# One attention kernel: value products of two key tiles issued together, every fourth score step, in the cosine half

## What is computed

```python
xn = layernorm(x)                                   # (2, 1024, 128), 16 heads of 8
q, k = l2norm(xn @ Wq.T), l2norm(xn @ Wk.T)         # cosine: every key counts
out = softmax(g_scale * q @ k.T) @ (xn @ Wv.T)
...
q, k = rope(rms(xn) @ wq), rope(rms(xn) @ wk)       # causal: 16 query, 4 key heads
out = softmax(mask(q @ k.T / sqrt(8))) @ (rms(xn) @ wv)
```

## Time and profile before

| | |
|---|---|
| Median of three runs | 706.77 us |
| The profiled execution, as a run | 705.19 us |
| Its span in the trace | 703.5 us |
| TensorE matmul busy | 620.3 us (88%) |
| ScalarE busy | 461.6 us (66%) |
| VectorE busy | 367.0 us (52%) |
| GpSimd busy | 103.9 us (15%) |
| Mean granted TensorE clock | 0.966 of 2.4 GHz |

### The profile page before, as it was taken

One profiled execution on the slowest core, in us unless ns is written; L12 is line 12 of the kernel. 1 busy time (PEld: TensorE's weight loads), 2 busy tenths in 40 slices (PEclk: granted clock), 3 DMA queues, 4 the chain that ended last, 5 costly groups with the idle time before them and its releaser, 6 DMA issues.

```text
span 703.5 us, 11087 instructions
## 1 busy us (share of the span) xinstructions
PE 620.3 (88%) x4068; PEld 272.4 (39%) x4068; DVE 367.0 (52%) x1042; ACT 461.6 (66%) x520; POOL 103.9 (15%) x245
## 2 busy tenths in 40 slices
PE   0661789999999999999999999999998689999996
PEld 0331223333333333333333333333333445556654
DVE  6577565555547465555555654655521534344333
ACT  1344548888889888888888888988988342222221
POOL 8245000210210210030021021021002200000000
PEclk9976779999999999999999999999999889999999
DMA  3015100320311302123332030221000000000000
GB/s 84 4 17 88 31 16 16 48 41 7 62 16 31 54 9 47 28 36 76 114 54 35 13 62 11 36 46 18 1 3 1 1 0 1 15 1 16 0 16 15
DMA packets 19189, 20.61 MB, mean 29 GB/s; under 512 B 8128, under 2 KB 15552, under 8 KB 19136
## 3 DMA queue, kind: packets, MB, share of 16 engines
q1 hardware_dynamic: 16736, 19.62, 15.9%
q10 hardware_dynamic: 2400, 0.30, 0.3%
HBM read 3.84 MB, written 1.05 MB: 7 GB/s over the span
## 4 chain that ended last, share of the span: by engine, by line
PE 78%; DVE 14%; ACT 5%; issue 2%; DMA 1%; SPq 0%; POOL 0%; DVEq 0%; ACTq 0%
PE ps L1050 27%; PE ps L1031 19%; PE ps L982 6%; PE ps L1127 6%; PE ps L1113 5%; PE ps L1114 5%; PE ps L1011 3%; DVE neg_piece L719 2%; DVE masked_scores L715 2%; PE ps L1005 2%; ACT probs L583 2%; DVE out_t L795 2%; DMA x_tok<-in_x 1%; DVE probs L692 1%; DVE probs L681 1%
## 5 line engine op out<-in xcount | busy, mean ns | idle before, releaser
L583 ACT ACTIVATE probs<-ps 128x1024 f32<-128x1024 f32 (+2 forms) x416 | 395.5, 991 | 77.6 <-PE ps L1031 73.4
L715 DVE CUSTOM_DVE_ANT_0 masked_scores<-ps,mask_q 128x384 bf16<-128x384 f32 (+3 forms) x256 | 111.6, 488 | 75.8 <-PE ps L982 75.3
L1050 PE MATMUL ps<-probs,v_cos_pad 128*32 128x512 f32 x1024 | 139.0, 615 | 0.0
L1031 PE MATMUL ps<-q_cos_t,k_cos_t 64*128 64x512 f32 x512 | 124.2, 482 | 16.6 <-DVE parts_rope L703 14.7
L1031 PEld LDWEIGHTS ps<-q_cos_t,k_cos_t 64*128 64x128 f32 x512 | 48.8, 188 | 137.4 <-ACT probs L583 74.5
L502 POOL TENSOR_SCALAR_AFFINE_SELECT probs<-probs 128x512 f32<-128x512 f32 x64 | 40.3, 635 | 413.6 <-ACT probs L583 413.6
L719 DVE TENSOR_REDUCE neg_piece<-ps 128x1 f32<-128x512 f32 x128 | 82.2, 685 | 20.3 <-PE ps L982 20.3
L621 ACT ACTIVATE probs<-ps 128x512 f32<-128x512 f32 x48 | 28.5, 597 | 96.3 <-PE ps L1114 84.9
L982 PE MATMUL ps<-k_causal_t,q_causal_t 33*128 33x512 f32 (+3 forms) x384 | 65.3, 378 | 19.9 <-DVE neg_piece L719 10.6
L1050 PE MATMUL ps<-probs,v_causal_pad 128*32 128x512 f32 (+3 forms) x768 | 81.6, 498 | 0.3 <-POOL probs L502 0.3
L1031 PE MATMUL ps<-q_causal_t,k_causal_t 64*128 64x512 f32 (+3 forms) x384 | 73.2, 406 | 3.2 <-ACT probs L583 3.2
(11 more groups left out here) (129 smaller groups left out, 412.6 us busy)
## 6 DMA issues: line engine op xcount, KB each, us to landing
q_cos_t<-parts_t_cos SPq DMA_DIRECT2D x64, 64.0 KB
q_causal_t<-parts_t_rope SPq DMA_DIRECT2D x64, 64.0 KB
k_cos_t<-parts_t_cos SPq DMA_DIRECT2D x32, 64.0 KB
k_cos_t<-parts_t_cos SPq DMA_DIRECT2D x64, 32.0 KB
parts_cos<-in_w SPq DMA_DIRECT2D x2, 768.0 KB, 5.6
x_tok<-in_x SPq DMA_DIRECT2D x4, 256.0 KB, 4.4
k_causal_t<-parts_t_rope SPq DMA_DIRECT2D x16, 64.0 KB
k_causal_t<-parts_t_rope SPq DMA_DIRECT2D x32, 32.0 KB
```

The lines of the kernel that those rows point to most:

```text
L583: act.activation(step_probs(n), step_scores(n), ACT.Exp).then_inc(probs_ready, 1)
L715: ins = dve.tensor_tensor_reduce(out=masked_scores[:, head % 2, at:at + keys], in0=scores, in1=mask_q[:, BANK - keys:BANK], scale=-1.0, sc ...
L1031: ins = pe.matmul(slot(n)[:, i, at:at + width], rounded(keys[:, j * P:(j + 1) * P]), rounded(queries[:, q0:q0 + width]), start=True, stop= ...
L1050: ins = pe.matmul(acc[32 * h:32 * h + 32, lo:], v, unit_probs(n)[:, h, lo:], start=j == 0, stop=True, skip_group_check=True)
```

## The change

`unit_steps` gives two consecutive cosine units (an even one and the odd one after it) the same step: two after the last score step of the odd one. `UNITS_AT` then holds a list of units for a step, and the loops of TensorE and VectorE go through the list. In every iteration the cosine pairs are due at relative steps 5, 9, 13, 17, 21, 25, 29 and 33. The causal units keep their steps, as do all jobs and `copy_sums` (steps 17 and 33 in the cosine). No instruction is added or removed on any engine; TensorE's order alone is another.

```diff
     for n in range(iters * UNITS_AN_ITERATION):
         it, u = divmod(n, UNITS_AN_ITERATION)
         step = it * STEPS + LAST_STEP[u] + (3 if on_diagonal(u) else 2)
-        if n:
+        if UNITS[u][0] == COS:
+            step = it * STEPS + LAST_STEP[u - u % 2 + 1] + 2
+        if n and not (UNITS[u][0] == COS and u % 2):
             step = max(step, at[-1] + (3 if UNITS[u][2] == 0 else 1))
         at.append(step)
...
-UNITS_AT = {step: n for n, step in enumerate(UNIT_STEP)}
+UNITS_AT = {}
+for _n, _step in enumerate(UNIT_STEP):
+    UNITS_AT.setdefault(_step, []).append(_n)
...
-                if n in UNITS_AT and UNITS_AT[n] % UNITS_AN_ITERATION in LAST_OF_HALF:
-                    copy_sums(UNITS_AT[n])
+                for u in UNITS_AT.get(n, []):
+                    if u % UNITS_AN_ITERATION in LAST_OF_HALF:
+                        copy_sums(u)
...
-                if n in UNITS_AT:
-                    value_unit(UNITS_AT[n])
+                for u in UNITS_AT.get(n, []):
+                    value_unit(u)
```

## The result

The changed kernel takes 740.36 us (median of four runs, 738.65 to 743.33) against 707.19 for the kernel before (median of four): a ratio of 1.0475, 95% interval 1.0441 to 1.051. It is slower by 33 us, where 742 was forecast. The profiled execution is the longest of the four, 743.33 us with a span of 741.6, so the two traces lie 38.1 us apart (703.5 before) where the medians lie 33 apart.

What follows compares the result with a forecast made beforehand. TensorE and ScalarE were taken to hold each other, with ScalarE's cover by two score slots too short for a pair. Iterations adding +27.5, +5.3 and +2.8 gave +35.6 us: 740.8 profiled, 742 median, range 734 to 754.

Steps and rivals of the forecast that it cites:

- The period: Four cosine score steps with one pair, replayed from the first scores after a pair: 4.92 us from start to start.
- idle time at a pair: ScalarE's wait from its last ready exponential to the first one after a pair: 1.14 us.
- the periods with transpositions: Four-step periods from step 22, with step 24's two transpositions, 5.45 us; from step 26, with jobs between scores, 5.13 us.
- The hold of a pair: Time two adjacent cosine value units keep TensorE from the next scores: 1.89 to 1.98 us, 1.90 used.
- The cover: ScalarE's ready work at a pair's start: 1.79 us from the start of scores 4, against 2.93 needed.
- the rival with TensorE as the pace: TensorE sets the pace and saved tiling-mode switches win 11.5 us: 695 us; chance 4%.
- The sums: Added time over all iterations: +27.5, +5.3 and +2.8 us, with 0 for the first iteration's early steps; together +35.6.
- Iterations 1 to 6: Steps 5 to 34 take 37.51 us against 32.92: +4.59 each, +27.5 in six.
- The last: Last iteration, which prepares no further queries and keys: 37.30 us against 31.96, +5.3.
- The first, from step 17: First iteration, steps 17 to 34: 22.3 us against 19.54, +2.8.
- Its steps 3 to 17: First iteration's early steps, paced by VectorE and partly at 1.2 GHz: change taken as 0, from -3 to +6 us.
- The clock: Rival: new TensorE gaps drop the clock to 1.2 GHz once per iteration, adding 27 us: 769 us; chance 8%.

Runs made afterwards that it cites:

- the catching up at step 7: Kernel before with single units re-placed by ScalarE's cover, two of them due together at step 7: 701.68 us; 700.57 us with the first iteration's order kept.

## Why the prediction was right

- **The period.** Worked out 4.92 us, measured 4.88; idle time at a pair 1.14 against 1.10; the periods with transpositions 5.45 against 5.41 (361.25 to 366.66 in the trace) and 5.13 against 5.02 (366.66 to 371.68). The order of steps in it, TensorE held by the pair, then ScalarE awaited twice, is that of the trace.
- **The hold of a pair.** 1.90 was taken between 1.89 and 1.98; it is 1.86 (349.63 to 351.49), a little under the lower end. In the trace the second unit starts 0.88 us behind the first. So a pair does save TensorE time. The Trainium skill (TensorEngine Tiling (Array Packing), Key Properties) has a change of the tiling mode drain the array; the trace agrees in sign, with 0.88 us from a unit to a unit and 0.98 from a unit to scores (340.76 to 341.74). By that rule alone the kernel would have won; the runs show that the time saved turned into waiting.
- **The cover.** The point from which pairs cost was put at a hold under 0.8 us. Holds of 1.86, 1.00 and 0.58 us gave idle times of 1.10, 0.25 and none, so at 1.86 us the rival with TensorE as the pace lost, on the side of the point that was named.
- **The sums.** Iterations 1 to 6: 4.59 each forecast, 4.2 measured (steps 5 to 34 take 37.12, forecast 37.51). The last: 5.3 forecast, 6.6 measured. The first, from step 17: 22.3 forecast, 22.05 measured. Its steps 3 to 17: taken as 0, from -3 to +6, measured +3.7 (33.92 against 30.21), at a mean clock of 0.62 where it had been 0.75. These errors cancelled in part: too much in the middle, too little at the ends. Between the two traces 38.1 us were added where 35.6 were forecast, and ScalarE's idle time rose by 43.3 where some 35 were. So the mechanism and the period were forecast; that the median came within 2 us of 742 is in part luck.
- **The clock.** Given 8% as one fall in each iteration. In iterations 1 to 7 of the profiled execution it fell once, in the last, which prepares nothing for a next iteration; the pair that it hit, and the one after it:

```profile
529.46 3.32 PE L1056 MATMUL ps<-probs,v_cos_pad 128*32 128x512 f32 x16
...
535.98 1.92 PE L1056 MATMUL ps<-probs,v_cos_pad 128*32 128x512 f32 x16
```

The pair that it hit took 3.32 us and steps 9 to 17 took 11.39 in place of 9.76, so 1.6 us, more than the 1.3 that the last iteration had over its forecast. As a price it was small here; with pairs and no maxima jobs on two slots, and with narrow pairs of 128 columns, it became large.

## What to carry to other kernels

An engine that feeds another through a few buffers must not do more of its other work in a row than the filled buffers cover: count the work that stands ready for the fed engine when the block starts (here 1.79 us from the last scores), and the time until the next item reaches it (issue, block and latency, 2.93 us). Beyond that point the time that merged blocks save comes back as waiting on both sides. Below it, merging cost nothing where it was measured (3.67 us in both orders at 128 columns), but apart from the catching up at step 7 no run here shows it winning. So look for another buffer first: a third slot, in kernels without the maxima jobs, took single units from 697.58 to 661.11 us. A busy share of 98% on one engine does not show which engine paces; the idle time of its partner right behind a block does.

## What the runs showed that was not expected

- The granted clock fell in kernels in which no wait of TensorE in iterations 1 to 7 is longer than 1.1 us: with two slots, pairs and no maxima jobs, twelve times in iterations 1 to 7, some 20 of the about 25 us that this kernel lost beyond the count. With narrow units of 128 columns in pairs, iterations 1 to 3 had a mean clock of 0.82 to 0.88 and took 57 to 58.5 us in place of the 53 of the later ones at full clock. The changed kernel has waits as long (up to 1.10 us) and kept the full clock through iterations 1 to 6; what decides is not shown.
- With three slots and single units the recorded lengths of the exponentials grew, from 1.02 us to 1.1 and more (a mean of 1032 ns over all of them, against 991), though their work is the same. Two in a row, late in a long run of queued exponentials:

```profile
309.84 1.18 ACT L582 ACTIVATE probs<-ps 128x1024 f32<-128x1024 f32 x1
310.74 1.19 ACT L582 ACTIVATE probs<-ps 128x1024 f32<-128x1024 f32 x1
```

They still start 0.90 us apart, as the shorter ones at the head of the run do, so ScalarE did not become slower: the records overlap more the longer the run of queued exponentials is. A pace is read from start to start and not from the length of a record.
